# Attention loop of a graph kernel: edge-major one-hots from small tables of targets, node-major ones by the transposing DMA

## The reference, cut to what matters

```python
h = jnp.einsum('nf,fhd->nhd', x, W)
a_src = jnp.sum(h * att_src, axis=-1)
a_dst = jnp.sum(h * att_dst, axis=-1)
e = jax.nn.leaky_relu(a_src[src] + a_dst[dst], NEG_SLOPE)
e_max = jax.ops.segment_max(e, dst, num_segments=N)
e_exp = jnp.exp(e - e_max[dst])
denom = jax.ops.segment_sum(e_exp, dst, num_segments=N)
alpha = e_exp / (denom[dst] + 1e-16)
...   # the messages alpha * h[src] are summed by dst
```

## Time and profile before

| what | value |
|---|---|
| time, median of 3 runs | 6537.67 us (6533.43 to 6541.74) |
| the profiled execution's own time | 6540.98 us |
| its span, first to last instruction | 6539.1 us |
| mean granted TensorE clock | 0.804 of full speed |
| busy: PE, VectorE, ScalarE, POOL | 74%, 55%, 27%, 33% |
| L1041 gathers | 1664, 1577.1 us busy |
| gat_targets broadcasts | 104 of 512.0 KB |

### The profile page before, as it was taken

How to read it: one execution, slowest core, us unless ns; L and a number is a source line. 1 busy time by engine, 2 the same in 40 slices (tenths; PEclk the granted TensorE clock), 3 DMA queues, 4 the chain that set the end, 5 groups by cost and what they waited for, 6 DMA issues and landing times. The chain is left out here.

```text
span 6539.1 us, 84391 instructions
## 1 busy us (share of the span) xinstructions
PE 4807.3 (74%) x25224; PEld 3437.6 (53%) x25225; DVE 3625.1 (55%) x7583; ACT 1736.2 (27%) x3028; POOL 2140.0 (33%) x2163
## 2 busy tenths in 40 slices
PE   1544676676666676767469963799999999977993
PEld 0432444444444444444358852566666666656873
DVE  6943454545454454545861137777777777763114
ACT  0022222222222222222112234333333333322121
POOL 1005566556566565656004423000000000021220
PEclk9986666666667766666679986899999999976997
DMA  3365455555555554545226661333333333332333
GB/s 88 63 217 124 128 138 130 137 131 138 130 135 134 129 136 128 138 129 133 65 66 207 208 205 54 80 78 82 74 75 74 80 80 74 75 88 95 106 120 102
DMA packets 1040972, 747.82 MB, mean 114 GB/s; under 512 B 815268, under 2 KB 926748, under 8 KB 1038717
## 3 DMA queue, kind: packets, MB, share of 16 engines
q1 hardware_dynamic: 937917, 457.79, 26.2%
q0 software_dynamic: 102848, 287.97, 16.6%
HBM read 480.57 MB, written 91.62 MB: 88 GB/s over the span
## 5 line engine op out<-in xcount | busy, mean ns | idle before, releaser
L1041 POOL DMA_INDIRECT gat_rows<-h_rows,gat_sources x1664 | 1577.1, 948 | 1061.9 <-issue 499.8
L1279 PE MATMUL gat_sum_ps<-gat_rows,gat_onehot 128*128 128x265 f32 x3328 | 1395.1, 576 | 469.5 <-issue 281.8
L1279 PEld LDWEIGHTS gat_sum_ps<-gat_rows,gat_onehot 128*128 128x128 f32 x3328 | 904.3, 286 | 744.4 <-issue 536.6
L1679 ACT CAST gnn_z<-build_ps 128x392 bf16<-128x392 f32 x1184 | 567.4, 486 | 1106.3 <-PE build_ps L1694 1095.7
L1694 PE MATMUL build_ps<-onehot_code,onehot_low 128*128 128x196 bf16 x4736 | 594.7, 250 | 158.0 <-DVE onehot_code L1621 138.7
L1704 PE MATMUL back_ps<-zb_pieces,gnn_z 128*128 128x384 bf16 x3626 | 672.8, 325 | 0.0
L1726 PE MATMUL front_ps<-x_res_wide,front_rows 128*128 128x448 bf16 x3108 | 669.3, 352 | 0.0
L1694 PEld LDWEIGHTS build_ps<-onehot_code,onehot_low 128*128 128x128 bf16 x4736 | 432.8, 98 | 334.8 <-issue 138.0
L1598 POOL DMA_INDIRECT front_rows<-zf_piece_rows,vrow_nodes x74 | 88.9, 1201 | 1555.3 <-PE front_ps L1726 1543.5
L1621 DVE TENSOR_TENSOR onehot_code<-dense_codes,code_pattern 128x1568 bf16<-128x1568 bf16 x592 | 573.6, 969 | 0.0
L1633 DVE TENSOR_TENSOR gnn_z<-gnn_z,front_ps 128x448 f32<-128x448 f32 x518 | 321.9, 621 | 398.7 <-PE front_ps L1726 398.5
(11 more groups left out here) (350 smaller groups left out, 5337.2 us busy)
## 6 DMA issues: line engine op xcount, KB each, us to landing
moe_w<-in_L_ffn_W SPq DMA_DIRECT2D x112, 512.0 KB
gat_targets<-gat_step_targets SPq DMA_DIRECT2D x104, 512.0 KB
moe_w<-in_L_ffn_w SPq DMA_DIRECT2D x32, 1024.0 KB
gat_rows<-h_rows,gat_sources POOLq DMA_INDIRECT x1664
moe_taken<-moe_rows_out SPq DMA_DIRECT2D x21, 896.0 KB, 7.1
moe_rows_out<-gat_slot_zeros SPq DMA_DIRECT2D x36, 512.0 KB
gat_flags<-gat_tile_flags SPq DMA_DIRECT2D x104, 128.0 KB
normal_rows<-moe_xn_all SPq DMA_DIRECT2D x14, 896.0 KB, 4.0
```

Of the source, the lines that this page charges most:

```text
L1041: pool.indirect_dma_start(out=g[:, b, t, :], out_offset=None, in_=T.h[:, :], in_offset=bass.IndirectOffsetOnAxis(ap=idx[:, b, t:t + 1], ax ...
L1279: last = pe.matmul(po[:, s % BANKS, 0:W], o[:, b, s * SUB + t, :], g[:, b, s * SUB + t, :], start=t == 0, stop=t == SUB - 1)
L1679: nc.scalar.copy(AT[:, k % 2, :, 2 * QUAD * c:2 * QUAD * (c + 1)].rearrange("p h (u d) -> p h u d", u=2), pb[:, c % 2, 0:2 * CW].rearrange ...
```

## The change

A new table `T.minus` holds the targets, relative to their window and with the sign turned, as one f32 for each edge, laid out as `T.idx` is. In `edge_tables` VectorE makes the values (one more pass for each `j`), PE transposes them with the sources, ScalarE copies them, and SyncE stores them in 112 more pieces of 8 KB, in turn with those of `T.idx`.

In the loop SyncE loads 8 KB of this table for each batch in place of the 512 KB broadcast. ScalarE makes the edge-major one-hots: 16 passes over 128x128, one for each tile, of abs(node number - target) with the target as bias of each partition, then relu(1 - distance) once in bf16 (`ob`) and once in f32 in place (`o`). The copy L1078 is gone. The transposing DMA now reads `ob` and writes `oT`, which has two buffers, and is issued one slot earlier (`turn(n-1)` in slot n); `dst_terms(n)` waits for it (`tr`) instead of `ot`. ScalarE no longer waits for `pv`; SyncE's turn does, for the batch before the last.

```diff
@@ edge_tables, SyncE
-                    sp.dma_start(T.idx[j * GS + m, :, :],
-                                 sx[:, j, m * STEPS:(m + 1) * STEPS, :].rearrange("p k t -> p (k t)")).then_inc(xs, 16)
+                    for rows, own in ((T.idx, sx), (T.minus, sn)):
+                        sp.dma_start(rows[j * GS + m, :, :],
+                                     own[:, j, m * STEPS:(m + 1) * STEPS, :].rearrange("p k t -> p (k t)")).then_inc(xs, 16)
@@ edge_tables, VectorE
+                dve.wait_ge(sd, j + 1)
+                dve.tensor_scalar(sr[:, j, 1, :, :], sr[:, j, 1, :, :], s0[:, j:j + 1], -1.0,
+                                  ALU.subtract, ALU.mult).then_inc(nl, 1)
@@ edge_tables, PE
-                for t in range(SUB):
-                    last = pe.transpose(px[:, t, :], sr[:, j, 0, t, :], C.ident[:, :])
+                pe.wait_ge(nl, j + 1)
+                for a in range(2):
+                    for t in range(SUB):
+                        last = pe.transpose(px[:, a, t, :], sr[:, j, a, t, :], C.ident[:, :])
@@ edge_tables, ScalarE
+                nc.scalar.copy(sn[:, j, :, :].rearrange("p k t -> p t k"), px[:, 1, :, :])
@@ gat_edges, SyncE
-            def turn(n):
+            def turn(n, a):
                 sp.wait_ge(ot, n + 1)
                 sp.nop(nofuse=True)
-                until(sp, oc, n)
+                until(sp, pv, n - 1)
                 sp.nop(nofuse=True)
-                sp.dma_start_transpose(ob[:, :, :], oT[:, :, :].rearrange("p t e -> p (t e)")).then_inc(tr, 16)
+                sp.dma_start_transpose(oT[:, a % 2, :, :], ob[:, :, :].rearrange("p t n -> p (t n)")).then_inc(tr, 16)
...
+                if a >= RING:
+                    sp.wait_ge(oc, n - (RING - 1))
+                    sp.nop(nofuse=True)
+                sp.dma_start(tgt[:, b, :], T.minus[bass.ds(n, 1), :, :].rearrange("a p t -> p (a t)")).then_inc(lk[b], 16)
...
-                if a >= 2:
-                    turn(n - 2)
+                if a >= 1:
+                    turn(n - 1, a - 1)
                     sp.nop(nofuse=True)
-                sp.dma_start(loc[:, b % 2, :], T.local[bass.ds(n * STEPS, STEPS), :].rearrange("k e -> (k e)").partition_broadcast(P))\
-                  .then_inc(lt[b % 2], 16)
@@ gat_edges, ScalarE
-            def turned_onehots(n, i, a):
-                act.wait_ge(lt[a % 2], (i * 2 + a % RING // 2) * 16 + 16)
-                until(act, tr, n * 16)
-                until(act, pv, n)
-                flat = oT[:, :, :].rearrange("p t e -> p (t e)")
-                nc.scalar.activation(loc[:, a % 2, :], loc[:, a % 2, :], ACT.Abs, bias=nodes[:, 0:1]).then_inc(ab, 1)
-                act.wait_ge(ab, n + 1)
-                nc.scalar.activation(flat, loc[:, a % 2, :], ACT.Relu, bias=C.one[:, 0:1], scale=-1.0).then_inc(ot, 1)
-
-            def onehots(n, a):
+            def onehots(n, i, a):
                 b = a % RING
+                act.wait_ge(lk[b], i * 16 + 16)
                 if a >= RING:
                     act.wait_ge(sc, n * STEPS - STEPS * (RING - 1))
-                act.wait_ge(tr, n * 16 + 16)
-                nc.scalar.copy(o[:, b, :, :], ob[:, :, :]).then_inc(oc, 1)
+                for t in range(TILES):
+                    last = nc.scalar.activation(o[:, b, t, :], C.iota[:, :], ACT.Abs, bias=tgt[:, b, t:t + 1])
+                last.then_inc(od, 1)
+                act.wait_ge(od, n + 1)
+                until(act, tr, n * 16)
+                flat = o[:, b, :, :].rearrange("p t e -> p (t e)")
+                nc.scalar.activation(ob[:, :, :].rearrange("p t n -> p (t n)"), flat, ACT.Relu, bias=C.one[:, 0:1],
+                                     scale=-1.0).then_inc(ot, 1)
+                nc.scalar.activation(flat, flat, ACT.Relu, bias=C.one[:, 0:1], scale=-1.0).then_inc(oc, 1)
@@ gat_edges, PE
-            def dst_terms(n, w):
-                pe.wait_ge(ot, n + 1)
+            def dst_terms(n, a, w):
+                pe.wait_ge(tr, n * 16 + 16)
```

More of the change, by code:

```diff
@@ L883, in _ @@
                 act.wait_ge(xp, j + 1)
-                nc.scalar.copy(sx[:, j, :, :].rearrange("p k t -> p t k"), px[:, :, :]).then_inc(xc, 1)
+                nc.scalar.copy(sn[:, j, :, :].rearrange("p k t -> p t k"), px[:, 1, :, :])
+                nc.scalar.copy(sx[:, j, :, :].rearrange("p k t -> p t k"), px[:, 0, :, :]).then_inc(xc, 1)
             for j in range(NJ):
@@ L912, in gat_edges @@
     li = k.sems("gat_sources_loaded", RING)
+    lk = k.sems("gat_minus_targets_loaded", RING)
     lg = k.sems("gat_flags_loaded", RING)
-    lt = k.sems("gat_targets_loaded", 2)
     ga = k.sems("gat_rows_gathered", RING)
-    ot = k.sem("gat_onehot_T_ready")
-    ab = k.sem("gat_distances_ready")
+    ot = k.sem("gat_onehot_bf_ready")
     tr = k.sem("gat_onehot_turned")
-    oc = k.sem("gat_onehot_copied")
+    od = k.sem("gat_onehot_distances_ready")
+    oc = k.sem("gat_onehot_ready")
     pv = k.sem("gat_dst_terms_ready")
@@ L1021, in slot @@
                 sp.dma_start(lst[:, b, :, :], T.least[:, bass.ds(n * TILES, TILES)].partition_broadcast(H)).then_inc(lg[b], 16)
-                if a >= 2:
-                    turn(n - 2)
+                if a >= 1:
+                    turn(n - 1, a - 1)
                     sp.nop(nofuse=True)
-                sp.dma_start(loc[:, b % 2, :], T.local[bass.ds(n * STEPS, STEPS), :].rearrange("k e -> (k e)").partition_broadcast(P))\
-                  .then_inc(lt[b % 2], 16)
-            rounds(sp, slot, 2)
+            rounds(sp, slot, 1)
         @block.gpsimd
@@ L1047, in _ @@
         def _(act):
-            act.wait_ge(cn, 7)
+            act.wait_ge(cn, 6)
             def src_terms(k, i, a):
@@ L1098, in _ @@
             dve.memset(minus[:, :], -1.0).then_inc(cn, 1)
-            dve.tensor_scalar(nodes[:, :], C.wiota[:, 0:1], -1.0, None, ALU.mult).then_inc(cn, 1)
             dve.memset(acc[:, :, :], 0.0).then_inc(cn, 1)
-            dve.wait_ge(cn, 7)
+            dve.wait_ge(cn, 6)
             dve.tensor_scalar(tsel[:, :], run[:, 0, 0:TILES], 0.0, None, ALU.is_le).then_inc(cn, 1)
             dve.tensor_scalar(run[:, 1, 0:TILES], run[:, 0, 0:TILES], -float(H), None, ALU.is_gt).then_inc(cn, 1)
+            dve.wait_ge(cn, 8)
+            dve.tensor_tensor(tsel[:, :], tsel[:, :], run[:, 1, 0:TILES], ALU.mult).then_inc(cn, 1)
             dve.wait_ge(cn, 9)
-            dve.tensor_tensor(tsel[:, :], tsel[:, :], run[:, 1, 0:TILES], ALU.mult).then_inc(cn, 1)
-            dve.wait_ge(cn, 10)
             dve.tensor_reduce(esel[:, :], C.ident[:, :].rearrange("p (t h) -> p h t", h=H), AX.X, ALU.add).then_inc(cn, 1)
             dve.wait_ge(wt, 16)
+            dve.wait_ge(cn, 11)
+            dve.tensor_copy(eselT[:, :], pXM[0:H, 0, :]).then_inc(cn, 1)
             dve.wait_ge(cn, 12)
-            dve.tensor_copy(eselT[:, :], pXM[0:H, 0, :]).then_inc(cn, 1)
-            dve.wait_ge(cn, 13)
             def totals(k, i, a):
@@ L1281, in scatter @@
                 last.then_inc(sc, 1)
-            def dst_terms(n, w):
-                pe.wait_ge(ot, n + 1)
+            def dst_terms(n, a, w):
+                pe.wait_ge(tr, n * 16 + 16)
                 until(pe, vr, n)
                 for t in range(TILES):
-                    last = pe.matmul(pV[:, t, :, :].rearrange("p s h -> p (s h)"), oT[:, t, :],
+                    last = pe.matmul(pV[:, t, :, :].rearrange("p s h -> p (s h)"), oT[:, a % 2, t, :],
                                      C.adst[:, bass.ds(w[t // SUB], 1), :].rearrange("p a h -> p (a h)"),
@@ L2259, in gnn_moe_kernel @@
         T.idx = k.dram("gat_batch_sources", [S.SG * P // STEPS, P, TILES], I32)
+        T.minus = k.dram("gat_batch_minus_targets", [S.SG * P // STEPS, P, TILES])
         T.local = k.dram("gat_step_targets", [S.SG * P, BLK], BF16)
```

22 lines of the change are left out of this document (11 added, 11 removed).

## The result

The changed kernel takes 6581.2 us (median of 5, 6565.5 to 6585.6) against 6533.4 for the kernel before (median of 5). The ratio is 1.0069, 95% interval 1.0052 to 1.0085: slower by 34 to 56 us. The profiled executions show the same, with spans of 6583.8 and 6539.1 us, 44.7 apart. The time lies inside the range that was given, 31 us above its likeliest value.

What follows compares the result with a forecast made beforehand. The loop was taken as bound by gathers (20.0 us a batch) plus PE's late answers, 25.3 us, unchanged. Tables +12.5 and loop 0 on a median of 6537.7 gave 6550 us; range 6420 to 6680 (0.79).

Steps and rivals of the forecast that it cites:

- the range that was given: Whole kernel: measured time between 6420 and 6680 us, given a chance of 0.79.
- The tables: Table stage, SyncE's queue: 112 more stores at 0.477 us delay the codes, so the stage ends 12.5 us later (0 to +34).
- VectorE's own addition: Table stage: 7 more passes of some 0.35 us, hidden under SyncE's queue; 2.5 us if the stores went away.
- D: Table stage: extra stores hidden because codes go out faster, loop unchanged; 6538 to 6541 us, chance 0.06.
- E: Table stage: each extra store paid until it lands, 2.0 us each, 224 us; 6745 us in all, chance 0.01.
- ScalarE's new work: Attention loop: 5.9 us a batch removed, 8.8 added; ScalarE busy 9.7 of 25.3 us (8.3 to 12.9), no bound.
- The slack of the transpose: Attention loop: transposing DMA issued at 1518.1, landing about 1523.3 or 1526; PE asks at 1535.22, leaving 9 us or more.
- The loop's term, 0: Attention loop: earlier transpose and removed broadcast change nothing, 0 us; start and end of the loop 0 plus or minus 2.
- rival C: Attention loop: PE's answers wait for the earlier transposing DMA, +2 to +5 us a batch; 6750 to 7050 us, chance 0.15.
- The reading of the stall: Attention loop: batch is 20.0 us gathers, 3.3 from last gather to PE's late answers, 2.0 to next gather: 25.3 us.
- rival B: Attention loop: late answers depend on the broadcast or ScalarE's wait for PE; 430 to 530 us saved, 6020 to 6120, chance 0.20.
- Its chances: Whole kernel against the one before: same 0.34, slower 0.46, faster 0.20, with about 0.2% (13.1 us) as the distinguishable difference.

## Why the prediction was right, and where it was off

**The tables** (+12.5 forecast). Codes from 312.3, measured 311.65; last issue 365.0, measured 364.7; next stage near 368, measured 368.34 for its first transfer, 12.2 us later than before. The loop began 9.6 us later in the profiled execution, and the run with the tables alone costs 10 to 25 us. The working of the queue held, and where the late answers are absent joining the stores took its cost away. Two things the sum had not reckoned with. VectorE's end at 354.5 hides 16 us of the queue; where it is earlier the same stores cost some 23 us. And VectorE's own addition, put at 2.5 us, measured 8.6 in the changed kernel (363.1) and 10.4 with the tables alone (364.9), against 0.8 on the chip without late answers; it stayed hidden under the queue, but without the queue it would be most of the cost. Rivals D (hidden) and E (224 us paid one by one) are out. The Trainium skill's rule to join small transfers, "DMA: Bandwidth & Descriptors", "Rules for kernel authors", is borne out as the repair. The price was 0.477 us a store and not the fixed cost of about 2.0 us, which that page's "Anatomy of one DMA" gives for DMAs that GpSimd issues; these are SyncE's.

**ScalarE's new work.** 16 short passes were put at 4.8 us; they take 4.77 (L1080 at 1508.43). ScalarE is busy for 184.28 of 500 us, 37%, where 9.7 of 25.3 is 38%. No bound, as forecast.

**The slack of the transpose.** Forecast: the bf16 one-hots 6.8 us after the short passes begin (1518.1 after 1511.30), transpose at once. Measured: 11.5 us after (1519.95 after 1508.43) and the transpose at 1520.63, as ScalarE's own semaphore came 4.7 us late, which the prediction had not thought of. Its 1526 for a landing of twice 2.0 us is 1525.2 by its own terms. The slack was still enough: PE waited for the transposed one-hots 13.6 us in all, in one place, by its list of waits.

**The loop's term, 0.** This is the step that was mis-sized: "the loop's term is 0" measured +34.5 us, 0.33 a batch. It had costed the earlier transpose by who waits for it, and found nobody. What the runs show is that the point at which SyncE issues it, with the loads behind it, costs by itself: 0.6 us ahead of VectorE's scan and 1.6 ahead of the restart of the gathers, a third of the batches are longer; 5 us later it costs nothing, with the same ScalarE work, the same tables and the same loads. Whether it is the transpose or the loads is open. The size is less than the smallest that rival C priced (1 us a batch, 6650), and it is not C's mechanism: C let PE's answers wait for the transpose's landing, and they come 3.3 us after the last gather's end with the early transpose as with the late one. What is longer is the time behind the answers. In the long batches PE has got less far when its answers stop: L1294 ends 9.4 us (median) before they come, in the batches with less than 4.4 us of idle time 11.8. Then VectorE's adds of steps 2 and 3 are caught, and the sums of steps 6 and 7 still stand when the answers come. How DMAs issued at the restart bring this about some 15 us later isn't shown, nor what makes answers late at all.

**The reading of the stall.** The prediction said: 20.0 of gathers, plus 5.3 that belong to late answers. The chips without late answers confirm the sum: 2083.8 us of loop instead of 2635.3, 20.0 us a batch, for a kernel of the same time as the kernel before. Its rival B had priced nearly this (430 to 530 us), but took the change for a possible cause; it comes and goes from one chip to another, and the change didn't take it away. That the answers come with the end of the gathers, 3.3 us after the last, was read from two batches; it holds over the whole loop, in this kernel and the changed one. The earlier trace rows has the exception that the prediction passed over: before that batch's own work begins, ScalarE and VectorE are released 10.6 us after the last gather's end, not 3.3. Its chances have a small slip: by its own terms same is 0.29 + 0.06 = 0.35 and slower 0.29 + 0.15 + 0.01 = 0.45, where it has 0.34 and 0.46.

## What to carry to other kernels

A DMA that nobody waits for can still cost by where in the batch it is issued, or by what its place does to the DMAs behind it: measure it at two places before calling it hidden, and move it alone. Stores of a few KB are paid per issue on the queue, some 0.48 us each here; the time they cost is what the queue exceeds the work beside it by, so count both ends. And a stall that is named after a releaser of a stage long past may not belong to the kernel at all: run the same program on a second chip before building on it. A delay that looks constant in one batch should be measured over all of them, from both of its possible causes.

## What the runs showed of the hardware

The same program, the kernel before, took 6533 to 6540 us in the first measurements and the first group of runs and 5964 to 5966 us in the last three groups, on three other chips. Each chip was measured once, so whether this is the chip or its state at that time is open. 551 us of the difference are in the loop, in answers by semaphore that come late while indirect gathers run: those of PE by some 10 us (4.9 to 14.6 in single batches of the changed kernel) and, but for the start, 3.3 us after the last gather of a batch ended. On the first kind they hit PE's semaphores and, in the changed kernel, ScalarE's semaphore to itself (4.7 us), and PE's own issue slows to one record in 2.9 us (1541.58, 1544.44). What does this isn't shown. TensorE's granted clock in the loop was 0.65 of full speed on the first and 0.79 on the others (PEclk of the run with POOL waiting for the adds):

```profile
1000.00:1500.00 500.00, 373.25 (x1521) 257.87 (x1521) 310.96 (x846) 169.05 (x175) 378.43 (x400) 0.79 0.64 168
```

Two stores of 128 KB in runs of 64 bytes occupied the issuing queue for some 4.5 us, with what the store behind them took longer; 32 of 8 KB, the same bytes, for 15.3.
